# A vision tower kernel: the experts' gate-scaled tokens are read from the SBUF copy of h3 transposed, not from a second transpose in PSUM

## The chip, the cores and the metric

The kernel runs on one core of a Trainium2 chip. The metric is device microseconds of one execution, median of three runs. All arithmetic is fp32.

## The reference, cut to what matters

64 images of 3x224x224 are cut into 14x14 patches, so T = 196 tokens of D = 256 features each. Two layers follow: a state-space mixer with a feed-forward part, then attention with a mixture of experts. The change concerns the last part, where `h3` is the normalised result of the attention:

```
h3  = layernorm(h2 + attention(h2))
gate = softmax(h3 @ Wg + bg); the two largest of 8 are kept and divided by their sum
out = sum over the 8 experts e of gate[e] * (h3 @ We[e].T + be[e])
result = layernorm(h3 + out)
```

The kernel multiplies the tokens by the gate first and then by the expert's weights: `acc += We[e] @ (h3T * gate[e])`.

## The kernel before, in words

Every image goes through the same list of steps, and the steps are placed in slots. There are 16 slots to an image, one for each group of the state scan (GROUPS = IC * GC = 4 * 4). The constants `AT_...` say in which slot of an image's own time a step is issued; slot 76 is slot 12 of the sixteen, four images later than the scan of that image. So at any time the engines work on up to nine images at once, and every engine issues its instructions in one fixed order. Where two engines meet, a semaphore holds the later one.

What fills a slot:

- POOL (GpSimd) makes the scan's input, `X = u * Bb` (`inputs`, L461), and after the scan the product `X = X * Cb` (`times_c`, L471). Both read two tensors in SBUF. It also does the small steps of the layernorms (L476 to L483).
- DVE (VectorE) runs the scan (L1066) on `X` in SBUF and the decay `dA` in PSUM.
- ACT (ScalarE) makes `dA` (L863), and most drains of PSUM and the exponentials (L897, L928, L935).
- PE (TensorE) sums the products over the states into the bank `YB` (`sum_states`, L576), and does all projections and transposes.

PSUM is rationed. Three banks G0, G1 and G2 and a pair S are each shared by up to a dozen uses in the order of their slots. A `Bank` counts fills and releases: a use waits (`free`) until the use before it has released the bank. G0 serves, among others, `qk` (slot 42, so 10 of 16), `h3T2` (76, so 12) and `values` (46, so 14).

The part around the change, in the sixteen slots of one round:

- Slot 0: PE turns `h3` into `h3T` (`turn`, L608), and ACT copies it to SBUF (`drain_turned`, L884) into one of two buffers `h3T[q % 2]`. The gate (L675) and later the residual (`add_residual`, L1191) read that copy.
- After the gate is worked out it goes through HBM and comes back spread over all partitions, as `Gb` (one DMA of 784 KB per image).
- Slot 12: PE turns `h3` a second time, into bank G0 as `h3T2` (L608 again). DVE then makes the scaled tokens of four pairs of experts, `hg` (`scale_pair`, L1182), pair 0 and 1 in slot 12, pair 2 in slot 13, pair 3 in slot 14. There are two `hg` buffers (GRING = 2), so pair 2 waits until PE has used pair 0. Behind pair 3 DVE waits for its own product and releases the bank (L1184, L1185).
- Slots 13, 13, 14 and 0: PE multiplies each pair by the experts' weights (`expert_pair`, L694), 16 matmuls to a pair.

Other steps that the text names, in the slots of the same round: the gate of the state-space input `gate_x` (L1045, slot 11 of its image's round) on DVE; the attention scores (L643) and the transposes of the probabilities (L653) on PE; `values` and the other token-major products (L616) on PE; the token mix (L1090) and the row maxima (L1113) on DVE; the step size `dt` (L1057) on DVE; `mv_y` (L1075), the moments of the scan's output, on DVE. L608 serves the transposes of `h1`, `h2`, `h3` and the second one of `h3`, four matmuls to each.

Of the kernel before, what the change touches and what calls it, by code (L numbers as in the profile page):

```python
# [11 lines left out]
P = 128  # L12
# [5 lines left out]
T = SIDE * SIDE  # L18
# [101 lines left out]
AT_WS_OUT = 72  # L120
AT_GATE_STORE = 71
AT_GATE_LOAD = 73
AT_H3T2 = 76
AT_SCALE = (76, 76, 77, 78,)
AT_PAIR = (77, 77, 78, 80,)
AT_ACC_OUT = 80
# [8 lines left out]
CYCLE = 4  # L135


G0_USES = {"k": AT_RK, "patch0": AT_PATCH[0], "v": AT_V, "moeT": AT_MOE_T, "AV2": AT_AV[2], "qk": AT_QK, "h3T2": AT_H3T2, "values": AT_VALUES}
G1_USES = {"h3T": AT_H3T, "gate": AT_GATE, "embed": AT_EMBED, "out": AT_OUT, "h1T": AT_H1T}
G2_USES = {"AV0": AT_AV[0], "patch2": AT_PATCH[2], "r": AT_RK, "xproj": AT_XPROJ, "patch1": AT_PATCH[1], "AV1": AT_AV[1], "ws": AT_WS, "h2T": AT_H2T, "AV3": AT_AV[3], "acc": AT_PAIR[0]}  # L140
S_USES = {"xb": AT_XB, "ln": AT_DT_OUT, "z": AT_Z, "turn_y": AT_TURN_Y, **{f"S{n}": AT_SCORES[n] for n in range(UNITS)},
# [43 lines left out]
def vit_tower(nc, x, w_tok, b_tok, w_in, conv_w, conv_b, w_xproj, a_log, d_par, dt_w, dt_b, w_out, ln_g, ln_b,  # L185
              w_r, w_k, w_v, mu_r, mu_k, w_qk, b_q, b_k, w_vv, b_v, gamma, w_g, b_g, w_e, b_e,
              ident, q_mask, k_mask, rank_of, proj, gates, out):
    with ExitStack() as ctx:
# [329 lines left out]
        def _(pe):  # L518
# [194 lines left out]
            def step(b, par):  # L713
                for g in range(GROUPS):
                    def at(slot):
                        return live(b, par, g, slot)

                    for s, q in at(AT_H3T2):
                        turn(s, "h3T2", h3)
                    for s, q in at(AT_TURN_Y):  # L720
                        turn_y(s)
                    for s, q in at(AT_V):
                        pe.wait_ge(ksq_ready, s + 1)
                        token_major(s, "v", ka, wv)
                    for s, q in at(AT_XPROJ):
                        xproj(s)
                    for s, q in at(AT_GATE):
                        gate(s, q)
                    for s, q in at(AT_MOE_T):
                        turn_moe(s)  # L730
                    for s, q in at(AT_QK):
                        queries_keys(s)
                    for s, q in at(AT_H3T):
                        pe.wait_ge(normed["att"], s + 1)
                        turn(s, "h3T", h3)
                    for p in range(PAIRS):
                        for s, q in at(AT_PAIR[p]):
                            expert_pair(s, p)
                    for s, q in at(AT_EMBED):
                        embed(s)  # L740
                    for part in range(3):
                        for s, q in at(AT_PATCH[part]):
                            patches(s, part)
                    for n in range(UNITS):
                        for s, q in at(AT_SCORES[n]):
                            scores(s, n)
                        for s, q in at(AT_TURN_P[n]):
                            turn_probs(s, n)
                        for s, q in at(AT_AV[n]):
                            mix_values(s, q, n)  # L750
                    for s, q in at(AT_WS):
                        turn_gates(s)
                    for k in range(GROUPS):
                        for s, q in at(k + 2):
                            sum_states(s, q, k)
                    for s, q in at(AT_Z):
                        project_in(s, hT[q], "z", IC)
                    for s, q in at(AT_XB):
                        pe.wait_ge(where["embed"].drained, where["embed"].count("embed", s))
                        project_in(s, hT[q], "xb", 0)  # L760
                    for s, q in at(AT_RK):
                        pe.wait_ge(mix_step, 4 * (s + 1))
                        token_major(s, "r", xr, wr)
                        mix_keys(s)
                    for s, q in at(AT_OUT):
                        project_out(s, q)
                    for s, q in at(AT_H1T):
                        pe.wait_ge(where["out"].drained, where["out"].count("out", s))
                        turn(s, "h1T", h1)
                    for s, q in at(AT_H2T):  # L770
                        pe.wait_ge(normed["ffn"], s + 1)
                        turn(s, "h2T", h2[q % 2])
                    for s, q in at(AT_VALUES):
                        token_major(s, "values", h2T, wvv)
# [6 lines left out]
        def _(act):  # L781
# [163 lines left out]
            def step(b, par):  # L945
                for g in range(GROUPS):
# [61 lines left out]
                        normalise(s, "y", ysb, ysb)  # L1008
                    for s, q in at(AT_ATT_NORM):
                        if s > 0:  # L1010
                            filled("h3T2", s - 1)
                        normalise(s, "att", att, h3)

            act.wait_ge(w_landed, W_ALL)
# [6 lines left out]
        def _(dve):  # L1021
# [148 lines left out]
                then(v.reciprocal(gs[:, 4, :], gs[:, 4, :]))  # L1170
                v.tensor_tensor(gw[:], hb, wide(4), ALU.mult).then_inc(bank.drained, 1)

            def scale_pair(s, p):

                bank = where["h3T2"]
                if p == 0:
                    dve.wait_ge(gates_landed, 16 * (s + 1))
                    filled("h3T2", s)
                after(dve, hg_used, PAIRS * s + p + 1 - GRING)
                h = bank.tile[:, 0:DC * T].rearrange("p (o c t) -> p o c t", o=1, c=DC).broadcast_to([P, 2, DC, T])  # L1180
                w = Gb[:, 2 * p:2 * p + 2, :].rearrange("p e (o t) -> p e o t", o=1).broadcast_to([P, 2, DC, T])
                v.tensor_tensor(hg[p % GRING][:], h, w, ALU.mult).then_inc(hg_ready, 1)  # L1182
                if p == PAIRS - 1:
                    dve.wait_ge(hg_ready, PAIRS * (s + 1))  # L1184
                    dve.sem_inc(bank.drained, 1)  # L1185

            def add_residual(s, q):
                o = filled("acc", s)
# [7 lines left out]
            def step(b, par):  # L1196
                for g in range(GROUPS):
                    def at(slot):
                        return live(b, par, g, slot)

                    for s, q in at(AT_TOP2):
                        gate_part(s, GIN)
                    for k in range(GROUPS):
                        for s, q in at(k):
                            scan_group(s, k)
                    for s, q in at(AT_MOE_NORM):
                        after(dve, out_landed, 16 * s)
                        normalise(s, "moe", lambda k: where["moeT"].tile[0:TB, k * D:(k + 1) * D], ob, where["moeT"].drained)
                    for s, q in at(AT_MOE_STATS):
                        o = filled("moeT", s)  # L1210
                        moments(s, "moe", lambda k: o[0:TB, k * D:(k + 1) * D])
                    for n in range(UNITS):
                        for s, q in at(AT_AV[n] + 1):
                            attended(s, q, n)
                    for s, q in at(AT_FFN_STATS):
                        dve.wait_ge(where["v"].drained, where["v"].count("v", s))
                        moments(s, "ffn", lambda k: rs[:, k, :])
                    for p in range(PAIRS):
                        for s, q in at(AT_SCALE[p]):
                            scale_pair(s, p)  # L1220
                    for s, q in at(AT_MIX):
                        token_mix(s)
                    for t, which in AT_TAPS.items():
                        for s, q in at(t):
                            taps(s, which)
                    for n in range(UNITS):
                        for s, q in at(AT_SCORES[n] + 2):
                            row_max(s, n)
                    for s, q in at(AT_GATE_X):
                        gate_x(s)  # L1230
                    for s, q in at(AT_OUT_NORM):
                        normalise(s, "out", lambda k: where["out"].tile[0:TB, k * D:(k + 1) * D], h1, where["out"].drained)
                    for s, q in at(AT_Z_OUT):
                        gate_z(s)
                    for s, q in at(AT_Y_STATS):
                        dve.wait_ge(y_drained, IC * (s + 1))
                        moments(s, "y", lambda k: ysb[:, k, :])
                    for s, q in at(AT_FFN):
                        ffn_sum(s)
                    for s, q in at(AT_ATT):  # L1240
                        dve.wait_ge(where["AV3"].drained, where["AV3"].count("AV3", s))
                        moments(s, "att", lambda k: att[:, k, :])
                    for s, q in at(AT_STEP):
                        step_size(s, q)
                    for s, q in at(AT_OUT_STATS):
                        o = filled("out", s)
                        moments(s, "out", lambda k: o[0:TB, k * D:(k + 1) * D])
                    for s, q in at(AT_ACC_OUT):
                        add_residual(s, q)
                    for s, q in at(AT_VALUES_OUT):  # L1250
                        add_value_bias(s, q)
                    for s, q in at(AT_GATE_IN):
                        gate_part(s, 0)
# [88 lines left out]
```

## Time and profile before

| | |
|---|---|
| median of 3 runs | 5642.31 us (5641.2 to 5642.68) |
| the profiled execution | 5639.12 us |
| its span, first to last instruction | 5637.3 us |
| mean granted PE clock | 0.889 of 2.4 GHz |
| PE / POOL / ACT / DVE busy | 88% / 77% / 70% / 67% |

The span is one execution as the hardware profiler saw it; 1.8 us of the execution's own time lie outside it. PE busy time is modelled at its ends. Idle time of an engine is given with what ended it.

### The profile page before, as it was taken

What the parts mean: (1) busy time and instruction counts of PE and PEld (TensorE: products, weight loads), DVE (VectorE), ACT (ScalarE), POOL (GpSimd) and SP (SyncE); (2) the same over time, 40 slices, a digit from 0 to 9 for tenths busy, and PEclk for the clock granted to TensorE, in tenths of its full rate; (3) what the DMA queues carried; (4) which work ended last, traced back from release to release, by engine and by line L of the source; (5) the groups of instructions that cost most, each with busy time, mean ns of one, the idle gap of its engine ahead of it and who ended that gap; (6) DMA issues with size and microseconds to landing.
All of it is one profiled execution on the core that took longest, in us unless ns stands there. A gap on an engine that the chain in (4) does not pass through costs nothing.

```text
span 5637.3 us, 91426 instructions
## 1 busy us (share of the span) xinstructions
PE 4983.9 (88%) x31232; PEld 4258.9 (76%) x31232; DVE 3802.5 (67%) x7568; ACT 3930.8 (70%) x9218; POOL 4336.8 (77%) x3272
## 2 busy tenths in 40 slices
PE   4788988989989989999889889889889898899897
PEld 4677777777777777777777777777777777777776
DVE  3667666677677667667667677676666766776763
ACT  4777667677677677676676676676776776776752
POOL 5978778778788787787787787787787787877850
PEclk8789989889889899899899899899898898898887
DMA  4222222222222222222222222222222222222110
GB/s 107 57 45 65 60 53 58 67 54 57 67 54 56 69 49 59 68 51 60 59 60 60 53 66 60 53 63 62 53 58 66 54 57 67 53 56 69 42 36 24
DMA packets 730351, 328.60 MB, mean 58 GB/s; under 512 B 631286, under 2 KB 655136, under 8 KB 729632
## 3 DMA queue, kind: packets, MB, share of 16 engines
q1 hardware_dynamic: 729888, 322.76, 23.5%
q8 instruction: 250, 4.10, 0.3%
q14 instruction: 213, 1.74, 0.1%
HBM read 307.75 MB, written 14.90 MB: 57 GB/s over the span
## 4 chain that ended last, share of the span: by engine, by line
PE 46%; DVE 27%; ACT 16%; issue 8%; POOL 2%; SPq 1%; DMA 0%; DVEq 0%; ACTq 0%; POOLq 0%
PE YB L576 12%; PE G L694 10%; DVE X L1066 9%; PE SB L643 5%; PE G L616 4%; PE SB L653 4%; DVE xbs L1037 4%; PE SB L553 3%; ACT dA L863 3%; ACT dt L844 2%; PE G L608 2%; ACT y L878 2%; PE G L561 2%; ACT xbs L812 2%; PE G L624 1%
## 5 line engine op out<-in xcount | busy, mean ns | idle before, releaser
L1066 DVE TENSOR_TENSOR_SCAN X<-dA,X 128x392 f32<-128x392 f32 x2048 | 1875.6, 957 | 839.1 <-ACT dA L863 805.6
L471 POOL TENSOR_TENSOR X<-X,Cb 128x784 f32<-128x784 f32 x1024 | 1893.8, 1849 | 4.6 <-DVE X L1066 4.2
L461 POOL TENSOR_TENSOR X<-u,Bb 128x784 f32<-128x784 f32 x1024 | 1891.6, 1847 | 4.6 <-DMA Bb<-proj_rows 4.6
L863 ACT ACTIVATE dA<-dt,negA 128x195 f32<-128x195 f32 x4096 | 1517.7, 417 | 272.0 <-DVE X L1066 245.8
L576 PE MATMUL YB<-idn,X 128*98 128x128 f32 x8192 | 1284.6, 311 | 28.9 <-POOL X L471 28.9
L576 PEld LDWEIGHTS YB<-idn,X 128*98 128x98 f32 x8192 | 1077.7, 147 | 166.3 <-issue 107.4
L694 PE MATMUL G<-hg,we 128*128 128x196 f32 x4096 | 772.7, 348 | 5.9 <-DVE hg L1182 5.9
L694 PEld LDWEIGHTS G<-hg,we 128*128 128x128 f32 x4096 | 737.4, 205 | 7.6 <-issue 6.0
L870 ACT ACTIVATE ysb<-YB 98x256 f32<-98x256 f32 x256 | 98.2, 384 | 742.8 <-PE YB L576 692.2
L643 PE MATMUL SB<-km,qm 32*98 32x392 f32 x1024 | 472.2, 588 | 148.9 <-DVE xbs L1045 142.3
L666 PE MATMUL G<-vs,pT 98*98 98x33 f32 x4096 | 406.0, 255 | 125.8 <-DVE att L1130 112.8
L666 PEld LDWEIGHTS G<-vs,pT 98*98 98x98 f32 x4096 | 387.9, 171 | 165.9 <-issue 158.3
L935 ACT ACTIVATE pr<-pr,nmx 98x196 f32<-98x196 f32 x1024 | 385.1, 450 | 106.6 <-DVE nmx L1113 96.0
L653 PE MATMUL SB<-idn,pr 98*98 98x98 f32 x2048 | 269.6, 285 | 202.6 <-DVE dt L1057 177.3
L476 POOL TENSOR_TENSOR veps_att<-mv_att,epsc 98x2 f32<-98x2 f32 x64 | 12.5, 195 | 553.6 <-DVE mv_att L1075 553.6
L1037 DVE SCALAR_TENSOR_TENSOR xbs<-SB,cw,xbs 128x195 f32<-128x195 f32 (+2 forms) x768 | 267.9, 411 | 245.3 <-ACT xbs L812 241.2
L653 PEld LDWEIGHTS SB<-idn,pr 98*98 98x98 f32 x2048 | 219.0, 148 | 242.2 <-issue 233.3
L553 PE MATMUL SB<-hT,win 128*128 128x196 f32 x2048 | 381.8, 341 | 16.2 <-ACT hT L803 8.5
L643 PEld LDWEIGHTS SB<-km,qm 32*98 32x98 f32 x1024 | 169.5, 181 | 295.3 <-issue 276.5
L553 PEld LDWEIGHTS SB<-hT,win 128*128 128x128 f32 x2048 | 355.1, 200 | 33.4 <-ACT pT L943 21.6
L1182 DVE TENSOR_TENSOR hg<-G,Gb 128x784 f32<-128x784 f32 x256 | 240.4, 960 | 195.8 <-PE G L694 191.4
L943 ACT ACTIVATE pT<-SB 98x784 f32<-98x784 f32 x256 | 209.4, 818 | 117.9 <-PE SB L653 76.4
(147 smaller groups left out, 7386.1 us busy)
## 6 DMA issues: line engine op xcount, KB each, us to landing
Bb<-proj_rows SPq DMA_DIRECT2D x256, 392.0 KB, 4.4
Cb<-proj_rows SPq DMA_DIRECT2D x256, 392.0 KB, 3.8
Gb<-gate_rows SPq DMA_DIRECT2D x64, 784.0 KB, 4.7
px<-in_x SPq DMA_DIRECT2D x1024, 36.8 KB
out<-ob SPq DMA_DIRECT2D x64, 196.0 KB
dtin<-proj_rows SPq DMA_DIRECT2D x64, 98.0 KB, 2.8
we<-in_w_e SPq DMA_DIRECT2D x1, 2048.0 KB
proj_rows<-pj SPq DMA_DIRECT2D x64, 25.3 KB
```

Of the source, the lines that this page charges most:

```text
L461: tt(X[(GROUPS * s + g) % RING][:], u[q % 2][:, c:c + 1, :].broadcast_to([P, NG, T]), Bb[:, NG * ng:NG * (ng + 1), :], ALU.mult).then_inc( ...
L471: tt(t[:], t[:], Cb[:, n0:n0 + NG, :], ALU.mult).then_inc(prod_ready, 1)
L553: last = mm(o[:, j // 2, (j % 2) * T:(j % 2 + 1) * T], lhsT=win[:, k, m * P:(m + 1) * P], rhs=src[:, k, :], start=(k == 0), stop=(k == DC ...
L576: last = mm(YB[0:TB, k * P:(k + 1) * P], lhsT=X[(GROUPS * s + g) % RING][:, j, k * TB:(k + 1) * TB], rhs=idn[:], is_transpose=True, start= ...
L643: last = mm(o[0:TB, j, :], lhsT=qm[:, n % 2, k * TB:(k + 1) * TB], rhs=km[:, 2 * j:2 * j + 2, :].rearrange("p h t -> p (h t)"), start=True ...
L653: last = nc.tensor.transpose(o[0:TB, j // 2, at:at + TB], pr[(UNITS * s + n) % PRING][:, j, k * TB:(k + 1) * TB], idn[:TB, :TB])
L666: last = mm(o[0:TB, j * (DV + 1):(j + 1) * (DV + 1)], lhsT=pT[:, j // 2, at:at + TB], rhs=vs[q % 2][:, k, h0 + j, :], start=(k == 0), stop ...
L694: last = mm(o[:, m * T:(m + 1) * T], lhsT=we[:, k, at:at + P], rhs=hg[p % GRING][:, e, k, :], start=(p == 0 and e == 0 and k == 0 and m == 0),
L863: last = go(dA[i % DRING][:, j, 1:T], dt_[q % 2][:, c, 1:T], ACT.Exp, scale=negA[:, c, n:n + 1])
L935: last = go(pr[i % PRING][:, j, :], pr[i % PRING][:, j, :], ACT.Exp, bias=nmx[i % PRING][:, j:j + 1])
L1037: last = v.scalar_tensor_tensor(out=xbs[:, c, k:], in0=S.tile[:, c // 2, at:at + T - k], scalar=cw[:, c, TAPS - 1 - k:TAPS - k], in1=xbs[: ...
L1066: v.tensor_tensor_scan(t, dA[i % DRING].rearrange("p n t -> p (n t)"), t, 0.0, ALU.mult, ALU.add).then_inc(scan_done, 1)
```

## The change

The second transpose is dropped, with its place in the order of G0. `scale_pair` reads the SBUF copy `h3T[q % 2]` instead, and waits for the drain of `h3T`. Since no bank is held any more, the wait behind pair 3 and the release go too. On ACT the attention's layernorm, which overwrites `h3`, waits for the first transpose of the image before and no longer for the second.

```diff
-AT_H3T2 = 76
...
-G0_USES = {... "qk": AT_QK, "h3T2": AT_H3T2, "values": AT_VALUES}
+G0_USES = {... "qk": AT_QK, "values": AT_VALUES}
...
-                    for s, q in at(AT_H3T2):
-                        turn(s, "h3T2", h3)
...
                         if s > 0:
-                            filled("h3T2", s - 1)
+                            filled("h3T", s - 1)
                         normalise(s, "att", att, h3)
...
-            def scale_pair(s, p):
-
-                bank = where["h3T2"]
+            def scale_pair(s, q, p):
+
                 if p == 0:
                     dve.wait_ge(gates_landed, 16 * (s + 1))
-                    filled("h3T2", s)
+                    dve.wait_ge(where["h3T"].drained, where["h3T"].count("h3T", s))
                 after(dve, hg_used, PAIRS * s + p + 1 - GRING)
-                h = bank.tile[:, 0:DC * T].rearrange("p (o c t) -> p o c t", o=1, c=DC).broadcast_to([P, 2, DC, T])
+                h = h3T[q % 2][:].rearrange("p (o c) t -> p o c t", o=1).broadcast_to([P, 2, DC, T])
                 w = Gb[:, 2 * p:2 * p + 2, :].rearrange("p e (o t) -> p e o t", o=1).broadcast_to([P, 2, DC, T])
                 v.tensor_tensor(hg[p % GRING][:], h, w, ALU.mult).then_inc(hg_ready, 1)
-                if p == PAIRS - 1:
-                    dve.wait_ge(hg_ready, PAIRS * (s + 1))
-                    dve.sem_inc(bank.drained, 1)
```

## Rows read from the trace of the kernel before

**Rows 1.** The page: busy time of PE, and the granted clock in 40 slices.

```profile
PE 4983.9 (88%) x31232; PEld 4258.9 (76%) x31232; DVE 3802.5 (67%) x7568; ACT 3930.8 (70%) x9218; POOL 4336.8 (77%) x3272
...
PEclk8789989889889899899899899899898898898887
```

**Rows 2.** Groups by line, whole span: busy us, mean ns, idle before by releaser.

```profile
L1182 DVE TENSOR_TENSOR hg<-G,Gb 128x784 f32<-128x784 f32 x256 | 240.4, 960 | 195.8 <-PE G L694 191.4 <-DMA Gb<-gate_rows 4.5
```

**Rows 3.** The chain in order of time, round near 2720 us: start us, us, what.

```profile
2710.10 0.99 DVE xbs L1045
...
2711.22 2.69 PE SB L643 x4
...
2716.44 6.29 PE G L694 x32
...
2728.31 0.88 DVE hg L1182
...
2737.92 0.48 DVE accT L1191
...
2738.54 1.51 PE G L616 x6
```

**Rows 4.** Timeline of PE, same round: start us, us, instruction, idle before.

```profile
2708.38 0.50 PE L608 MATMUL G<-idn,h 98*128 98x98 f32 x4
2711.22 2.69 PE L643 MATMUL SB<-km,qm 32*98 32x392 f32 x4 [2.33 <-DVE xbs L1045]
...
2726.19 1.55 PE L643 MATMUL SB<-km,qm 32*98 32x392 f32 x4
...
2729.29 1.97 PE L616 MATMUL G<-wvv,h2T 128*98 128x256 f32 x8 [0.32 <-DVEq L1185]
```

**Rows 5.** Timeline of DVE, same round.

```profile
2713.64 1.83 DVE L1182 TENSOR_TENSOR hg<-G,Gb 128x784 f32<-128x784 f32 x2
...
2720.12 0.97 DVE L1182 TENSOR_TENSOR hg<-G,Gb 128x784 f32<-128x784 f32 x1 [2.91 <-PE G L694]
...
2728.23 0.95 DVE L1182 TENSOR_TENSOR hg<-G,Gb 128x784 f32<-128x784 f32 x1
2729.33 0.75 DVE L1090 SCALAR_TENSOR_TENSOR xr<-G,mur,xr 128x196 f32<-128x196 f32 x2
```

**Rows 6.** Timeline of POOL, same round.

```profile
2711.86 1.84 POOL L461 TENSOR_TENSOR X<-u,Bb 128x784 f32<-128x784 f32 x1
2722.22 0.20 POOL L476 TENSOR_TENSOR veps_att<-mv_att,epsc 98x2 f32<-98x2 f32 x1 [8.53 <-DVE mv_att L1075]
...
2727.19 1.85 POOL L471 TENSOR_TENSOR X<-X,Cb 128x784 f32<-128x784 f32 x1
2729.00 1.85 POOL L461 TENSOR_TENSOR X<-u,Bb 128x784 f32<-128x784 f32 x1
```

**Rows 7.** Stretches: busy time by engine (instructions), granted PE clock, DMA share, GB/s.

```profile
2711.43:2718.26 6.83, 6.83 (x23) 4.93 (x22) 5.78 (x8) 1.54 (x4) 2.27 (x2) 0.50 0.30 110
...
2776.28:2783.11 6.83, 5.24 (x28) 5.20 (x29) 4.71 (x8) 6.16 (x14) 5.31 (x3) 0.50 0.52 149
...
2796.76:2803.59 6.83, 6.73 (x21) 4.81 (x22) 6.09 (x8) 1.54 (x4) 2.60 (x2) 0.50 0.34 121
5015.43:5022.26 6.83, 6.83 (x22) 4.87 (x23) 5.95 (x8) 1.54 (x4) 2.44 (x2) 0.50 0.32 116
```

**Rows 8.** Waits, whole span: us in total, times, longest us.

```profile
PE SB L653 <- DVE dt L1057: 177.3, 60, 3.1
...
DVE X L1066 <- POOL X L461: 30.4, 21, 2.4
```

**Rows 9.** Timeline of DVE: one instruction in three rounds running.

```profile
3091.40 0.25 DVE L1075 BATCH_NORM_AGGREGATE mv_y<-stat_y 98x2 f32<-98x6 f32 x2
...
3177.06 0.25 DVE L1075 BATCH_NORM_AGGREGATE mv_y<-stat_y 98x2 f32<-98x6 f32 x2
...
3262.17 0.25 DVE L1075 BATCH_NORM_AGGREGATE mv_y<-stat_y 98x2 f32<-98x6 f32 x2
```

More of the change, by code:

```diff
@@ L135 @@
 CYCLE = 4
-G0_USES = {"k": AT_RK, "patch0": AT_PATCH[0], "v": AT_V, "moeT": AT_MOE_T, "AV2": AT_AV[2], "qk": AT_QK, "h3T2": AT_H3T2, "values": AT_VALUES}
+G0_USES = {"k": AT_RK, "patch0": AT_PATCH[0], "v": AT_V, "moeT": AT_MOE_T, "AV2": AT_AV[2], "qk": AT_QK, "values": AT_VALUES}
 G1_USES = {"h3T": AT_H3T, "gate": AT_GATE, "embed": AT_EMBED, "out": AT_OUT, "h1T": AT_H1T}
@@ L1219, in step @@
                         for s, q in at(AT_SCALE[p]):
-                            scale_pair(s, p)
+                            scale_pair(s, q, p)
                     for s, q in at(AT_MIX):
```

## The prediction

> **What bounds the kernel now.** I read the page first. No engine is full: PE is busiest, and its granted clock is below full speed in nearly every slice [rows 1]. So I went to the chain that ended last, in order of time, for a round in mid-run [rows 3]. The reader is to see that it changes engine all the time: DVE `xbs` (L1045), then PE without a gap through the scores (L643) and two expert pairs (L694), then ACT and DVE, where pair 3 of `hg` lies on it at 2728.31, then `accT` at 2737.92, and PE's L616 at 2738.54. A round takes 85.3 us: PE's low stretches below lie 5015.43 - 2711.43 = 2304.00 us apart over 27 rounds, which is 85.33 each [rows 7]. What is worth something is therefore not busy time but a piece of this chain.
>
> Next the timelines of PE, DVE and POOL around the change [rows 4 to 6], and then the granted clock by stretches [rows 7]. The clock decides this case. PE stands idle for 2.33 us before the scores at 2711.22 [rows 4], and from 2711.43 to 2718.26 the granted clock is 0.50, the lower of its two levels, 1.2 GHz. A round later the same stretch is 2796.76 to 2803.59, 85.33 us on, and 27 rounds later 5015.43 to 5022.26, to the hundredth at the same place [rows 7]. A second such stretch is 2776.28 to 2783.11, where PE has waited for DVE's `dt`; that wait comes 60 times [rows 7, 8]. So the low stretches recur every 85.33 us exactly, and do not move with the small jitter of the work.
>
> **What that does to a delay.** Four matmuls of the scores take 2.69 us inside the low stretch and 1.55 us outside it [rows 4]. If PE's wait ends d later while the low stretch stays where it is, d less of its work is done at half speed, and it finishes only about d/2 late. The trace has the trial of it. `mv_y` comes at 3091.40, 3177.06 and 3262.17 [rows 9]. The first interval is 85.66, so that round was 0.33 late against 85.33; the second is 85.11, so 0.22 of the 0.33 had been given back one round later, and 0.11 was left, a third. A delay d in every round then adds up to d / (1 - 1/3) = 1.5 d once, and costs nothing in each round after.
>
> **The change part by part.**
>
> *The second transpose goes from PE.* It is four matmuls, 0.50 us, at 2708.38 [rows 4]. Right behind it PE idles 2.33 us for DVE's `xbs`, so the wait grows to 2.8 us and the chain does not move: 0. Without that cover it would be 64 x 0.50 = 32 us, 0.6%. PE's wait before the scores stays on the side of idleness, so I expect the low stretch behind it as before.
>
> *The waits for the bank go.* `values` (L616) waits 0.32 us for DVE's release at L1185 [rows 4]; it becomes free to start 0.32 earlier. DVE itself stands still behind pair 3: from the start at 2728.23 to `xr` at 2729.33 are 1.10 us, while pairs 0 and 1, one behind the other, take 1.83 together [rows 5], which with the length of 0.95 leaves 0.88 from start to start. So DVE gains 1.10 - 0.88 = 0.22. Both branches meet at L616 of 2738.54, which starts 0.14 behind the end of `accT` (2737.92 + 0.48) [rows 3]: the DVE branch ends last, and the chain gains 0.22 a round.
>
> *ACT's wait* for the first transpose of the image before, 12 slots earlier than the second was, can't be later than the old one: 0. G0 has one use less, `values` follows `qk`, which the scores already needed: 0. No DMA is added or moved. `scale_pair`'s wait for the drain of `h3T` is for something the gate has long read: 0.
>
> *`hg` from SBUF.* 256 products now read both inputs from SBUF, 4 a round. One with an input in PSUM takes 960 ns [rows 2]. The trace has no large DVE product with both inputs in SBUF, so the instruction alone I leave at 960. What is open is what happens beside POOL, which reads two SBUF tensors in each of its products. Pair 0 starts at 2713.64, POOL's L461 ends at 2711.86 + 1.84 = 2713.70: 0.06 at most, with L694 not due before 2716.44. Pairs 1 (2714.5) and 2 (2720.12) fall into POOL's idle time of 8.53 us that ends at 2722.22: 0 [rows 3, 5, 6]. Pair 3 at 2728.23 falls into L471, 2727.19 to 2729.04, with L461 right behind it at 2729.00 [rows 5, 6]. This one is on the chain [rows 3]. Bounds: 0, if the two don't touch, and 0.81 if DVE waits until L471 has ended. A further POOL product before DVE gets its turn would make 0.81 + 1.85 = 2.66. I take 0.81, the end that my forecast must survive; behind pair 3 on DVE are `xr`, `xk`, a row maximum and the scan, and ACT and PE wait for those, so all of it counts. POOL, held up for at most 0.96, has room: DVE waited for its `X` 21 times in the run, out of 2048 scans [rows 8].
>
> By the Trainium skill (SBUF — State Buffer, § Who interferes with whom) a DVE instruction with two SBUF inputs contends with a GpSimd instruction that reads SBUF, and whoever comes second is blocked until the other ends. No row here shows it; by that page the term is the 0.81, without it 0.
>
> **The sum** per round is 0.81 - 0.22 = +0.59 with the wait and -0.22 without it. POOL has products to make in about 59 of the 64 rounds with a pair 3, the others are the tail. Taken straight through that is +35 us or, over 64 rounds, -14 us. By the clock's give-back it is a single shift of 1.5 x 0.59 = 0.9 us, and the round stays 85.33. The profiled execution's 5639.1 us would become 5640.0; against the median of 5642.3, 3.2 us above it, I say 5643.
>
> **The rivals.** A difference below 0.2% (11 us) can't be told from no change here.
>
> 1. *No change: the rounds stay tied to the low stretches* (60%). For it: 27 rounds to the hundredth [rows 7], and the give-back after a delay [rows 9]. Against it: a constant lateness of 0.9 us is more than the 0.33 that I have seen given back. 5643 us, 5634 to 5653.
>
> 2. *Slower: pair 3 waits for POOL and it is not given back* (25%). Place: DVE, slot 14, the product beside L471. Price: +0.59 in 59 rounds, 5642.3 + 35 = 5677 us. It decides where PE's waits end so late that the falls of the clock behind them come at another place, or that the low stretch holds no more work to give back; the low stretch is 6.83 us, so that point is unknown but not before the 0.3 us seen. Half of it given back ends at 5660. If DVE lost a second POOL product each time, it would be 2.66 - 0.22 = 2.44 a round, 5786 us, which I give no more than 3 in 100 and leave outside the range.
>
> 3. *Faster: the two engines don't touch* (15%). The chain is 0.22 shorter, and rounds that come early are not held back: the give-back works on lateness only. 5642.3 - 14 = 5628 us. If the clock holds the round here too, it is case 1. The missing transpose may add a little in the tail, where PE has no queue.
>
> **How the numbers follow.** The time is that of case 1, 5643. Its own range is 5634 to 5653. The range of 8 in 10 reaches to the price of case 2 at its top and to case 3 at its foot: 5626 to 5678. Chances: faster 0.15, within 0.2% 0.60, slower 0.25.
>
> **What would show it in the profile after.** L608 is down to 768 matmuls, and PE's wait for `xbs` (L1045) is some 0.5 us longer with the scores at 0.50 clock still. L616 has no wait for DVE's queue. DVE's group of `hg` has a pair 3 that starts late or lasts up to 1.8 us where the other three keep 0.96: then the two engines touch; POOL's product behind it starts or ends up to 0.96 late. Low stretches still recur at 85.33 us, with the work lying some 0.9 us later against them. Wrong would be: low stretches at other distances than 85.33 (case 2, or a new pattern with a time of its own), four products of 0.96 (no contention), or a wait of DVE for POOL's `X` that grows with each round.

## The result, and the profile after

The changed kernel takes 6055.35 us (6054.89 to 6056.01, 4 runs) where the kernel before takes 5641.76 beside it (5640.81 to 5642.68). That is 1.0734 times as long, with a 95% interval of 1.072 to 1.0747: 7.3% slower, 414 us. The prediction said 5643, within 5626 to 5678.

The groups by line after, as in [rows 2], with POOL's two products beside them:

```profile
L470 POOL TENSOR_TENSOR X<-X,Cb 128x784 f32<-128x784 f32 x1024 | 1893.0, 1849 | 308.4 <-DVE X L1063 308.2
...
L1178 DVE TENSOR_TENSOR hg<-h3T,Gb 128x784 f32<-128x784 f32 x256 | 607.2, 2392 | 193.3 <-PE G L693 189.7
```

The product `hg` took 960 ns on average; now it takes 2392. POOL's own product lasts what it did, but POOL now stands idle for 308 us in front of it, waiting for DVE's scan. The view of the one line says how the 2392 are made up (ns, smallest, median, largest):

```profile
L1178 DVE TENSOR_TENSOR hg<-h3T,Gb x256: 947/974/7046, 410.3 to 6039.9; 128x784 f32<-128x784 f32 x128
```

194 of the 256 are as fast as before (under 1.1 us), 59 last 7 us, and three lie between, at 3.42 to 4.08 us. The timeline of DVE in the round that answers to [rows 5] shows which:

```profile
2713.82 1.84 DVE L1178 TENSOR_TENSOR hg<-h3T,Gb 128x784 f32<-128x784 f32 x2
...
2720.30 0.98 DVE L1178 TENSOR_TENSOR hg<-h3T,Gb 128x784 f32<-128x784 f32 x1 [2.89 <-PE G L693]
...
2728.42 7.04 DVE L1178 TENSOR_TENSOR hg<-h3T,Gb 128x784 f32<-128x784 f32 x1
2735.38 0.74 DVE L1087 SCALAR_TENSOR_TENSOR xr<-G,mur,xr 128x196 f32<-128x196 f32 x2
```

It is pair 3, as foreseen, but with 7.04 us and not 1.8. POOL in the same round, against [rows 6]:

```profile
2727.36 1.87 POOL L470 TENSOR_TENSOR X<-X,Cb 128x784 f32<-128x784 f32 x1
2729.18 1.86 POOL L460 TENSOR_TENSOR X<-u,Bb 128x784 f32<-128x784 f32 x1
2730.98 1.85 POOL L470 TENSOR_TENSOR X<-X,Cb 128x784 f32<-128x784 f32 x1
2732.78 1.85 POOL L460 TENSOR_TENSOR X<-u,Bb 128x784 f32<-128x784 f32 x1
2739.72 1.84 POOL L470 TENSOR_TENSOR X<-X,Cb 128x784 f32<-128x784 f32 x1 [5.09 <-DVE X L1063]
```

Pair 3 starts while the first of these runs. Three more POOL products, back to back, go ahead of it. They end at 2732.78 + 1.85 = 2734.63, and pair 3 ends 0.83 later, at 2735.46. POOL has stopped there only because its next product waits for a scan that is queued on DVE behind pair 3. So DVE waited until POOL had nothing left that it could do. It is the same in every round: each of the 62 slow products ends 0.83 to 0.84 us after the end of a POOL product behind which POOL stops.

PE meets it next, and its clock with it (timeline of PE, then the stretches; columns as in [rows 4] and [rows 7]):

```profile
2730.72 1.04 PE L575 MATMUL YB<-idn,X 128*98 128x128 f32 x8
2736.98 0.89 PE L607 MATMUL G<-idn,h 98*128 98x98 f32 x4 [5.22 <-DVEq L1091]
```

```profile
2711.72:2718.55 6.83, 6.83 (x23) 5.13 (x22) 5.69 (x7) 1.54 (x4) 2.18 (x2) 0.50 0.31 103
2735.62:2742.45 6.83, 5.47 (x19) 5.50 (x20) 5.42 (x9) 4.52 (x12) 2.73 (x2) 0.50 0.19 62
2803.88:2810.71 6.83, 6.64 (x21) 4.72 (x22) 6.19 (x9) 1.54 (x4) 2.67 (x2) 0.50 0.40 118
```

PE stands idle for 5.22 us in a place where it did not before, and late in that idle time, at 2735.62, a new stretch at 1.2 GHz begins. The stretch of [rows 7] that begins after the wait for `xbs` is still there (2711.72), and the next one begins at 2803.88: a round is now 92.16 us in place of 85.33, 6.83 longer. Of that, pair 3 explains directly: from its start to `xr` are 2735.38 - 2728.42 = 6.96 us, before they were 1.10 [rows 5], so 5.86.

### The profile page after: what moved, and what is told of

Same layout as the page of the kernel before. It is cut to its first block, busy times and chain, and to the rows that moved or that the text cites. A ratio compares the mean times of both kernels' runs of the same rounds, so it can differ in the third digit from the quotient of the medians.

```text
span 6053.5 us, 90850 instructions
## 1 busy us (share of the span) xinstructions
PE 5074.0 (84%) x30976; PEld 4353.5 (72%) x30976; DVE 4166.9 (69%) x7568; ACT 3929.9 (65%) x9218; POOL 4336.7 (72%) x3272
## 4 chain that ended last, share of the span: by engine, by line
PE 43%; DVE 32%; ACT 15%; issue 7%; POOL 2%; SPq 1%; DMA 0%; DVEq 0%; ACTq 0%; POOLq 0%
PE G L693 11%; PE YB L575 10%; DVE X L1063 9%; DVE hg L1178 7%; PE SB L642 5%; PE SB L652 4%; DVE xbs L1034 3%; PE SB L552 3%; ACT dA L860 3%; PE G L607 2%; PE G L615 2%; ACT dt L841 2%; ACT y L875 2%; PE G L560 1%; ACT xbs L809 1%
## 5 line engine op out<-in xcount | busy, mean ns | idle before, releaser
L470 POOL TENSOR_TENSOR X<-X,Cb 128x784 f32<-128x784 f32 x1024 | 1893.0, 1849 | 308.4 <-DVE X L1063 308.2
L460 POOL TENSOR_TENSOR X<-u,Bb 128x784 f32<-128x784 f32 x1024 | 1891.6, 1847 | 3.7 <-DMA Bb<-proj_rows 3.7
L575 PE MATMUL YB<-idn,X 128*98 128x128 f32 x8192 | 1267.5, 308 | 28.8 <-POOL X L470 28.8
L693 PE MATMUL G<-hg,we 128*128 128x196 f32 x4096 | 897.9, 386 | 15.9 <-DVE hg L1178 15.9
L693 PEld LDWEIGHTS G<-hg,we 128*128 128x128 f32 x4096 | 867.2, 235 | 17.9 <-issue 15.8
L1178 DVE TENSOR_TENSOR hg<-h3T,Gb 128x784 f32<-128x784 f32 x256 | 607.2, 2392 | 193.3 <-PE G L693 189.7
L652 PE MATMUL SB<-idn,pr 98*98 98x98 f32 x2048 | 292.0, 302 | 202.7 <-DVE dt L1054 176.9
L607 PE MATMUL G<-idn,h 98*128 98x98 f32 x768 | 163.7, 367 | 310.6 <-DVEq L1091 308.6
L652 PEld LDWEIGHTS SB<-idn,pr 98*98 98x98 f32 x2048 | 239.3, 158 | 242.3 <-issue 233.3
```

Of the source, the lines that this page charges most:

```text
L460: tt(X[(GROUPS * s + g) % RING][:], u[q % 2][:, c:c + 1, :].broadcast_to([P, NG, T]), Bb[:, NG * ng:NG * (ng + 1), :], ALU.mult).then_inc( ...
L470: tt(t[:], t[:], Cb[:, n0:n0 + NG, :], ALU.mult).then_inc(prod_ready, 1)
L575: last = mm(YB[0:TB, k * P:(k + 1) * P], lhsT=X[(GROUPS * s + g) % RING][:, j, k * TB:(k + 1) * TB], rhs=idn[:], is_transpose=True, start= ...
L652: last = nc.tensor.transpose(o[0:TB, j // 2, at:at + TB], pr[(UNITS * s + n) % PRING][:, j, k * TB:(k + 1) * TB], idn[:TB, :TB])
L693: last = mm(o[:, m * T:(m + 1) * T], lhsT=we[:, k, at:at + P], rhs=hg[p % GRING][:, e, k, :], start=(p == 0 and e == 0 and k == 0 and m == 0),
```

## The experiments

**Is it the operand? (e1)** The second transpose, its bank, its waits and its release stay; only the product reads SBUF:

```diff
-                h = bank.tile[:, 0:DC * T].rearrange(...)
+                h = h3T[q % 2][:].rearrange("p (o c) t -> p o c t", o=1).broadcast_to([P, 2, DC, T])
```

> The second transpose, its bank, its wait and its release all stay as in the kernel before; only the product reads h3T from SBUF. Theory A (two SBUF inputs on DVE against POOL): pair 3 still lasts about 7.0 us and the time is that of the changed kernel, 6055 us, within 15. Rival B (the freed bank and the missing transposes changed the order in which engines meet, and that brought the stall): all four pairs last 0.96 and the time is 5642.

Measured: 6063.59 us (6062.36 to 6064.9), 1.0757 of before (1.0742 to 1.0772). The operand alone brings the whole loss. With the transposes and the bank's waits kept, the time is some 8 us longer than that of the changed kernel, 0.1 to 0.2%.

**Does POOL stand in the way, and would a pause be enough? (e2)** One wait is put on POOL, in the slot behind pair 3:

```diff
+                    for s, q in at(AT_SCALE[3] + 1):
+                        pool.wait_ge(hg_ready, PAIRS * (s + 1))
                     for k in range(GROUPS):
                         for s, q in at(k - 1):
                             inputs(s, q, k)
```

> The changed kernel, with one wait on POOL: before its first product of the slot after pair 3 it waits until the four pairs of that image are made. Theory A (DVE gets the port when POOL has nothing ready behind its running product): pair 3 lasts 0.8 + 0.95 = 1.75 us instead of 7.0, POOL waits about 0.96, and the chain is 0.59 us a round longer than before the change. If a constant delay is given back by the clock, 5643 us; if not, 5677. Rival B (DVE waits for something else than POOL, such as a scan or ACT's step): pair 3 still lasts 7 us, 6055.

Measured: 5775.18 us (5770.03 to 5775.46), 1.0243 of before (1.0229 to 1.0257). DVE and POOL in one round (timelines):

```profile
2781.53 1.63 DVE L1180 TENSOR_TENSOR hg<-h3T,Gb 128x784 f32<-128x784 f32 x1
```

```profile
2780.46 1.86 POOL L470 TENSOR_TENSOR X<-X,Cb 128x784 f32<-128x784 f32 x1
2783.23 1.86 POOL L460 TENSOR_TENSOR X<-u,Bb 128x784 f32<-128x784 f32 x1 [0.91 <-DVE hg L1180]
```

Pair 3 now waits for one POOL product only, which ends at 2782.32, and ends 0.84 later. Theory A holds for the stall. `xr` starts at 2783.08, 1.55 behind the start of pair 3 against 1.10 [rows 5], so the delay on the chain is 0.45 us a round. But the time is 98 us above my higher figure of 5677: something was still missing, and it is taken up below.

**All four pairs in POOL's idle time (e3).** A third `hg` buffer lets pair 2 be made at once and pair 3 a slot earlier; PE's order is unchanged:

```diff
-GRING = 2
+GRING = 3
-AT_SCALE = (76, 76, 77, 78,)
+AT_SCALE = (76, 76, 76, 77,)
-        stat = {n: sb(f"stat_{n}", [TB, BLK, 6]) for n in LN}
+        stat = dict.fromkeys(LN, sb("stat", [TB, BLK, 6]))
```

> The changed kernel with three hg buffers; pairs 0, 1 and 2 are made in slot 12 and pair 3 in slot 13, all in POOL's idle time of 8.5 us; the small statistics tile is shared to make room. Theory A: all four products last 0.96 and none is late. The chain loses pair 3 (0.88) and the wait behind it (0.22) against the kernel before, 1.10 a round: 5570 us if all of it counts, 5642 if the rounds stay tied to the low stretches of the clock. Rival B (SBUF reads of h3T are slow in themselves, wherever they stand): products of several us in slot 12 too, over 6000 us.

Measured: 5560.81 us (5548.21 to 5564.62), 0.9861 of before (0.9848 to 0.9875). In its timeline of DVE, three pairs take 2.72 us together, and pair 3 falls into POOL's idle time too:

```profile
2753.11 2.72 DVE L1178 TENSOR_TENSOR hg<-h3T,Gb 128x784 f32<-128x784 f32 x3
...
2759.59 0.97 DVE L1178 TENSOR_TENSOR hg<-h3T,Gb 128x784 f32<-128x784 f32 x1 [2.01 <-PE G L693]
```

```profile
2751.35 1.83 POOL L460 TENSOR_TENSOR X<-u,Bb 128x784 f32<-128x784 f32 x1
2761.70 0.19 POOL L475 TENSOR_TENSOR veps_att<-mv_att,epsc 98x2 f32<-98x2 f32 x1 [8.51 <-DVE mv_att L1072]
```

Reading `h3T` from SBUF is as fast as reading PSUM when POOL is idle: three products of 0.97 us each in 2.72 us are 0.88 us from start to start, as in [rows 5]. The time is some 9 us below the 5570 that was expected at the least; the last experiment (e11) comes back to this order.

**What decides how long DVE waits?** Two variants of the changed kernel. In one (e7), pair 3 is made one slot later, behind scan 15:

```diff
-AT_SCALE = (76, 76, 77, 78,)
+AT_SCALE = (76, 76, 77, 79,)
```

> The changed kernel with pair 3 made one slot later, behind scan 15. Theory A (DVE gets its second input only when POOL stands at a wait): the product lasts until POOL has run out at the product behind scan 0, which is queued behind it on DVE: 5 to 6.5 us, and the time stays above 5950. Rival B (the 7 us belong to slot 14, where pair 3 meets ACT's and PE's steps): about 1 to 1.8 us.

Measured: 6075.24 us, one run. DVE and POOL in one round:

```profile
2828.18 6.48 DVE L1178 TENSOR_TENSOR hg<-h3T,Gb 128x784 f32<-128x784 f32 x1
```

```profile
2831.96 1.87 POOL L460 TENSOR_TENSOR X<-u,Bb 128x784 f32<-128x784 f32 x1
2836.49 1.85 POOL L470 TENSOR_TENSOR X<-X,Cb 128x784 f32<-128x784 f32 x1 [2.66 <-DVE X L1063]
```

Theory A holds. POOL runs out at 2833.83; pair 3 ends at 2834.66, again 0.83 later. In the round before, a gap of 0.07 us between two POOL products was enough: L470 had ended at 2739.44, L460 started at 2739.51 and lasted 2.46 us instead of 1.85, and pair 3 was through after 4.70 (POOL, then DVE):

```profile
2737.59 1.85 POOL L470 TENSOR_TENSOR X<-X,Cb 128x784 f32<-128x784 f32 x1
2739.51 2.46 POOL L460 TENSOR_TENSOR X<-u,Bb 128x784 f32<-128x784 f32 x1
```

```profile
2735.57 4.70 DVE L1178 TENSOR_TENSOR hg<-h3T,Gb 128x784 f32<-128x784 f32 x1
```

In another round, at 1165.92, it was let in after 4.67 us where the records show no gap at all (L470 ends at 1169.75, L460 starts at 1169.74 and lasts 2.56). So a gap in the record is a sign of an opening and not its measure.

In the other (e8), each POOL product is made as two instructions:

```diff
+                for h in range(2):
+                    last = tt(t[:, HALF * h:HALF * (h + 1), :], t[:, HALF * h:HALF * (h + 1), :],
+                              Cb[:, n0 + HALF * h:n0 + HALF * (h + 1), :], ALU.mult)
+                last.then_inc(prod_ready, 1)
```

and likewise for `X = u * Bb`.

> The changed kernel with each of POOL's products made as two instructions of 392 elements. Theory A (a product of DVE waits until POOL has no ready instruction, however many there are): pair 3 still lasts about 7 us. Rival E (DVE loses a fixed number of turns, four instructions in the changed kernel): it lasts 0.4 + 3 x 0.93 + 0.95 = about 4 us.

Measured: 6058.49 us, one run. Pair 3 is longer, not shorter, in part because POOL's work is a little longer in halves (two of them 1.99 to 2.01 us, one whole product 1.85):

```profile
2735.48 7.89 DVE L1184 TENSOR_TENSOR hg<-h3T,Gb 128x784 f32<-128x784 f32 x1
```

So it is not a number of turns that DVE loses. As long as POOL's instructions follow each other without a pause, they go first.

**A delay of known size.** The other half of the prediction was that a delay here costs nothing. In the kernel before, with its PSUM operand, the product of pair 3 is made more than once, at first twice (e4):

```diff
+                if p == PAIRS - 1:
+                    v.tensor_tensor(hg[p % GRING][:], h, w, ALU.mult).then_inc(again, 1)
+                    dve.wait_ge(again, s + 1)
                 v.tensor_tensor(hg[p % GRING][:], h, w, ALU.mult).then_inc(hg_ready, 1)
```

> The kernel before, with the product of pair 3 made twice from PSUM, one behind the other: a delay of known size, about 0.95 to 1.1 us a round, at the place where the changed kernel stalls. If a constant delay is given back by the clock's low stretches, as the prediction had it: 5643 to 5645 us, rounds of 85.33 us. If not: 64 x 1.0 = 64 us more, 5706. If the rounds jump to the next distance at which they tie to the clock, more than that.

Measured: 5642.85 us (5637.98 to 5645.7), 1.0007 of before (0.9998 to 1.0016): no change. Start of pair 3 to `xr` is 2729.92 - 2727.82 = 2.10 us against 1.10 [rows 5], a delay of 1.00 us in every round. And the round is still 85.33 us long (the stretch behind the wait for `xbs`, in two rounds running):

```profile
2727.82 0.95 DVE L1184 TENSOR_TENSOR hg<-G,Gb 128x784 f32<-128x784 f32 x1
2728.80 0.97 DVE L1186 TENSOR_TENSOR hg<-G,Gb 128x784 f32<-128x784 f32 x1
2729.92 0.75 DVE L1091 SCALAR_TENSOR_TENSOR xr<-G,mur,xr 128x196 f32<-128x196 f32 x2
```

```profile
2710.80:2717.63 6.83, 6.80 (x21) 4.87 (x22) 6.01 (x8) 1.54 (x4) 2.52 (x2) 0.50 0.30 120
2796.13:2802.96 6.83, 6.80 (x21) 4.87 (x22) 6.02 (x8) 1.54 (x4) 2.53 (x2) 0.50 0.30 120
```

The delay is given back, but at another place than the prediction had it. A round has a third low stretch, 3.41 us long, which the prediction did not list. In the kernel before it begins at 2762.63, behind PE's wait of 1.86 us for `att`, the output of the attention. In e4 it begins at 2748.34, ahead of that wait. PE in the kernel before:

```profile
2760.26 1.54 PE L666 MATMUL G<-vs,pT 98*98 98x33 f32 x16 [1.86 <-DVE att L1130]
...
2763.06 1.91 PE L576 MATMUL YB<-idn,X 128*98 128x128 f32 x8
...
2766.07 0.46 PE L532 MATMUL G<-idn,px 84*128 84x84 f32 x4
```

PE in e4:

```profile
2749.99 2.77 PE L617 MATMUL G<-wv,ka 128*98 128x256 f32 x8
...
2760.49 1.54 PE L667 MATMUL G<-vs,pT 98*98 98x33 f32 x16 [0.52 <-DVE att L1131]
...
2763.28 1.04 PE L577 MATMUL YB<-idn,X 128*98 128x128 f32 x8
...
2765.15 0.46 PE L533 MATMUL G<-idn,px 84*128 84x84 f32 x4
```

And the stretches, the first from the kernel before, the other two from e4:

```profile
2762.63:2766.04 3.41, 3.41 (x21) 3.37 (x20) 2.95 (x7) 2.18 (x5) 3.41 (x3) 0.50 0.00 0
```

```profile
2748.34:2751.75 3.41, 3.41 (x15) 2.82 (x13) 3.09 (x11) 3.41 (x10) 3.27 (x5) 0.50 0.14 29
2762.63:2766.04 3.41, 2.87 (x29) 2.49 (x29) 3.19 (x7) 2.78 (x8) 3.37 (x3) 1.00 0.02 5
```

In e4 the slow work stands ahead of the wait for `att` and is covered by it: the wait shrinks from 1.86 to 0.52 us. The work behind the wait, which was slow before, now runs at the full clock, and L577 takes 1.04 us instead of 1.91. Counted from the start of the stretch behind `xbs` (2711.43 before, 2710.80 in e4), PE's `att` work starts 0.86 late, at 49.69 against 48.83, and L533 starts 0.29 early, at 54.35 against 54.64. So the delay is gone within the round that it arose in. Over 25 rounds in mid-run PE's wait before `values` is 1.34 us on average against 0.32, its wait for `att` 0.64 against 1.86, and the low stretches together are as long as before, 17.2 us a round against 17.1. Why the stretch moves was not tested.

Made three times, in the same way (e10):

> The kernel before with the product of pair 3 made three times: a delay of 1.9 to 2.1 us a round, twice that of e4, which cost nothing. If the give-back by the clock's low stretches holds this as well: 5645 to 5650, rounds of 85.33. If it is used up, what is over counts in full, or the rounds go to the next distance: 5700 to 5850.

Measured: 5847.83 us (5844.45 to 5848.54), 1.0369 of before (1.0355 to 1.0383). The delay is 2736.43 - 2733.32 - 1.10 = 2.01 us, and the round goes to 2804.96 - 2716.21 = 88.75 us. It has one more low stretch, which begins at 2736.69, where PE has just started again after 2.34 us of waiting before `values` (2736.40):

```profile
2733.32 1.96 DVE L1185 TENSOR_TENSOR hg<-G,Gb 128x784 f32<-128x784 f32 x2
...
2736.43 0.75 DVE L1091 SCALAR_TENSOR_TENSOR xr<-G,mur,xr 128x196 f32<-128x196 f32 x2
```

```profile
2716.21:2723.04 6.83, 6.64 (x21) 4.71 (x22) 6.18 (x9) 1.54 (x4) 2.68 (x2) 0.50 0.42 120
2736.69:2740.10 3.41, 3.41 (x11) 2.31 (x10) 3.26 (x7) 1.11 (x4) 2.84 (x2) 0.50 0.98 341
2804.96:2811.79 6.83, 6.65 (x21) 4.72 (x22) 6.17 (x9) 1.55 (x4) 2.66 (x2) 0.50 0.33 120
```

Made seven times (e12):

> The kernel before, PSUM operand, transposes and bank kept, with the product of pair 3 made seven times: pair 3 to `xr` takes about 6 us more, near the 5.86 that the changed kernel loses there, and no DVE product shares anything with POOL. If the 7.3% is that delay on the chain, with the rounds going to the same distance of 92.16 us: 6055, within 20. If POOL's being held up had a part in it, or the delay alone costs only its own length: 5642 + 59 x 6 = 5996 or less.

Measured: 6073.79 us (6072.02 to 6075.48), 1.0768 of before (1.075 to 1.0786). From the first of the seven at 2729.65 to `xr` at 2736.80 are 7.15 us, a delay of 6.05, next to the 5.86 of the changed kernel. The round is the same as well: from `xr` at 2736.80 to `xr` at 3105.44 are four rounds of 92.16 us. So the 7.3% needs neither the SBUF operand nor any contention with POOL: a plain delay of the same size at the same place does it. It takes 18 us more than the changed kernel, and that lies in the tail. The last `xr` starts at 5915.52 here and at 5917.67 in the changed kernel; from there to the end of the span are 157.1 and 135.8 us. Three images have their pairs made in that stretch, where the changed kernel has no stall, and pay the delay here, 3 x 6.05 = 18.2 us.

**Why e2 cost 133 us and e4 nothing.** The delay of e2, 0.45 us, is less than half that of e4. In e2, 35 of the 63 steps from one `xr` to the next are over 87 us, most of them 88.5; in the kernel before none is. Two things had gone from PE in e2 that e4 still has: the four transposes, and the wait of `values` for the bank. First the transposes come back, with bank and waits, POOL yielding as in e2 (e5):

> POOL yields to pair 3 as in e2, but the second transpose stays on PE with its bank, wait and release, though no product reads it. e2 took 5775 us where a delay of 0.95 us a round cost nothing in e4. Theory C (the 0.5 us of transposes before PE's wait for xbs is what keeps the clock's pattern; without it there are more low stretches): the rounds are 85.33 us again and the time is 5643 to 5650. Rival D (POOL's own wait of about 1 us in every round is what costs): 5775, within 15.

Measured: 5654.48 us (5653.16 to 5656.74), 1.0022 of before (1.0013 to 1.0031). 121 us are gone by putting work and a wait back, though the time stays just above the 5650 that Theory C allowed. Then, in the kernel before, three of the four matmuls of the second transpose are left out (e6):

```diff
-                for m in range(DC):
-                    for k in range(BLK):
+                for m in range(1 if name == "h3T2" else DC):
+                    for k in range(1 if name == "h3T2" else BLK):
```

> The kernel before, but of the second transpose only one of the four matmuls is made, so three quarters of the tokens that the products read are whatever the bank holds; everything else, PSUM operand and waits too, stays. Theory C (less PE work before the wait for xbs changes the clock's pattern): more low stretches than the 1249 us of the kernel before, and a time clearly above 5642, up to 5740. Rival D (the transposes are covered and cost or save nothing, as the prediction had it): 5642, within 10.

Measured: 5642.25 us (5637.32 to 5644.55), 0.9999 of before (0.999 to 1.0008). Three quarters of the transposes go and the time does not change; the mean granted clock is 0.888 against 0.889 in the kernel before. That speaks against Theory C, but in a kernel without the delay at pair 3. The next run tests it with the delay. It is e2 with the wait alone put back, and still no second transpose (e9):

```diff
+                    for s, q in at(AT_SCALE[3]):
+                        pe.wait_ge(hg_ready, PAIRS * (s + 1))
                     for s, q in at(AT_VALUES):
                         token_major(s, "values", h2T, wvv)
```

> e2 (POOL yields, no second transpose) with one wait more on PE: before `values` it waits for pair 3, as it did when the bank had to be released. In e2 PE's waiting stood in one piece before L616 of `r` (1.18 us), and a low stretch of the clock followed it in most rounds; in e5 it stood before `values` (1.0 us) and the rounds stayed near 85.33. Theory F (the removed wait at `values` moved PE's idle time to a place where it brings the clock down): about 5650, within 15. Rival C (the missing 0.5 us of transposes does it): 5775.

Measured: 5651.39 us (5650.37 to 5652.93), 1.0021 of before (1.0012 to 1.003). No step from `xr` to `xr` is over 87 us any more. It was the wait, and not the transposes. Without it PE runs ahead through `values` and pair 3, and its idle time comes in front of L616 of `r` instead, here L617 (e2, timeline of PE, then the stretch):

```profile
2782.10 1.89 PE L617 MATMUL G<-wvv,h2T 128*98 128x256 f32 x8
...
2791.92 3.60 PE L617 MATMUL G<-wr,xr 128*98 128x256 f32 x8 [0.85 <-DVE accT L1186]
```

```profile
2791.88:2795.29 3.41, 3.37 (x8) 2.41 (x9) 2.43 (x3) 1.67 (x4) 3.41 (x3) 0.50 0.29 86
```

The granted clock falls to 0.50 just as PE starts again, and the product of `r` takes 3.60 us. With the transposes and the wait in place (e5, timeline of PE) the idle time stands in front of `values`, and the product of `r` takes 1.94:

```profile
2729.39 1.97 PE L618 MATMUL G<-wvv,h2T 128*98 128x256 f32 x8 [0.99 <-DVEq L1188]
...
2738.28 1.94 PE L618 MATMUL G<-wr,xr 128*98 128x256 f32 x8
```

**Does SBUF help in the better order?** The kernel before, PSUM operand and all, in the order of e3 (e11):

> The kernel before, PSUM operand and second transpose kept, with three hg buffers and pairs 0 to 2 in slot 12, pair 3 in slot 13, as in e3 (5561 us). If e3 gained by taking pair 3 off the chain: 5555 to 5575 here too. If reading from SBUF and the missing transpose and waits had a part in it: 5580 to 5640.

Measured: 5540.45 us (5527.42 to 5549.6), 0.9824 of before (0.9808 to 0.984). This is 15 us below the range that was expected. The gain of e3 is the order's, together with the third buffer and the shared statistics tile, which both kernels have and which were not tested apart. With the bank and the second transpose it is at least as fast as without, 0.4% lower in the ratio; what makes that small difference was not looked for. The rounds don't shorten evenly: `xr` comes at 2683.94, 2765.57 and 2851.20, so rounds of 81.63 and 85.63 us alternate, 83.63 on average.

## Why the prediction was wrong, point by point

**What bounds the kernel.** Right. Pair 3 lies on the chain; a delay of 2 or 6 us at that place comes out in every round (e10, e12), and the order that makes it earlier gave 1.4 to 1.8% (e3, e11).

**The transposes at 0.** Right: e6 removes three quarters of them for no change. In the changed kernel PE's wait for `xbs` is 2.67 us against 2.33, 0.34 longer and not 0.5.

**The waits for the bank, a gain of 0.22 a round.** Right as a size: in the changed kernel `xr` starts 0.08 before pair 3's record ends (2735.38 against 2735.46), where it had been 0.15 behind. The other wait, at `values`, I had counted as a gain that did not reach the end of the chain. With a delay behind pair 3 its removal is a loss of 124 us (e2 against e9), since it moves PE's idle time to where the clock falls behind it. In the changed kernel itself, with the large stall, this did not show: keeping waits and transposes there made it 8 us slower (e1).

**`hg` from SBUF, the step that failed.** Which pair is hit was right: pairs 0, 1 and 2 are as before, pair 3 waits. What failed is the size, "0.81 if DVE waits until L471 has ended". The wait was the rest of that product and three whole products more, 6.96 - 0.88 = 6.08 us. With the 0.22 taken off, the sum's +0.59 a round was +5.86. I had a bound of 2.66 for one further product and gave it 3 in 100. The row that should have warned was in the list: POOL's L461 starts at 2729.00, before L471 has ended at 2729.04 [rows 6]. POOL never pauses there, so whether DVE gets in between was the whole question, and the bound was POOL's queue up to its next wait for DVE, not the instruction that happens to run. e2, e7 and e8 show that rule from three sides.

By the Trainium skill (SBUF — State Buffer, § Who interferes with whom) the second of the two is blocked until the first finishes. The runs agree that they block each other: DVE waits where its product starts while one of POOL's runs, and in e7 POOL's L460 lasts 2.46 us instead of 1.85 where DVE is let in ahead of it. They differ in the price: DVE was not let in when the first POOL product ended, but stayed blocked through three more, 6.08 us in all. The measurement decides.

**The give-back.** Right in what it forecast for a small delay, wrong in how. 1.00 us a round costs nothing (e4), and the 0.45 of POOL yielding costs 0.2% where PE's idle time stays before `values` (e9); why this smaller delay is not free as well is open. The prediction had the delay given back at the scores, because they lie in the low stretch behind `xbs`, with the work standing 1.5 times the delay late against that stretch. In e4 the scores start 0.24 later against it than before (0.03 behind its start, where they were 0.21 ahead), not 1.5, and most of the delay is given back behind the wait for `att`, by the third low stretch, which the prediction left out. That the round stayed at 85.33 with 1.00 us was in this respect luck. The give-back has an end that the trace of before does not show: at 2.01 us the round is 3.42 longer, more than the delay itself (e10), and the 5.86 us of the changed kernel made it 6.83 longer.

**The rivals.** The second named the right place and pair with the wrong price. Its tail, 5786 us for one further POOL product, was the way to the truth, and the forecast stopped there. The third, that the two engines don't touch, is refuted by e1.

## What to carry to other kernels

Before an operand of a DVE instruction moves from PSUM to SBUF, look whether GpSimd reads SBUF at that moment, and how long it will go on without a pause: that whole run, up to its next wait, is the price, not the one instruction. Put such products where GpSimd waits anyway; here that order gained 1.4%, and with the PSUM operand 1.8%.

In this kernel, whose rounds are tied to PE's low-clock stretches, a delay on the chain cost nothing (1.00 us) or more than itself (2.01 us), and the removal of a wait cost 2%. So in such a kernel measure a known delay at the place (the same product twice) before pricing an edit there.

## What the runs showed of the hardware that was not expected

A DVE product with both inputs in SBUF starts, by the record, and then stands while GpSimd products that read SBUF follow each other without a gap: through four products in 7.04 us, through the ends of eight half products in 7.89. In e7 it is let in at a gap of 0.07 us in one round and with no gap in the record in another. It ends 0.83 to 0.84 us after the last of them. The record counts all of it as busy time of DVE.

The round of this kernel took 85.33 us with a delay of 0 and of 1.00 us, 88.75 with 2.01, and 92.16 with 5.86 (the changed kernel) and 6.05 (e12).
